# Adding an output bias to a residual held in SBUF: three VectorE additions, or two accumulating transfers that GpSimd begins

## What is computed

```python
h = concatenate([tokens(x), txt], axis=1)             # (16, 165, 256)
h = h + attn(layernorm(h))                            # y[..., None] * gelu(z) @ W_out + b_out
h = h + experts0(layernorm(h))                        # 8 experts, top 1 group, top 2
h = h + causal_attention(layernorm(h))
h = h + experts1(layernorm(h))                        # 4 experts, top 2
```

## Time and profile before

| | |
|---|---|
| Median of three runs | 919.74 us |
| The profiled execution: its time | 918.1 us |
| Its span, from the first to the last instruction | 916.1 us |
| TensorE busy | 779.2 us, 85% of the span |
| VectorE busy | 526.0 us, 57% |
| ScalarE busy | 361.0 us, 39% |
| GpSimd busy | 377.3 us, 41% |

### The profile page before, as it was taken

One profiled execution on the slowest core, in us unless ns is written; L12 is line 12 of the kernel. 1 busy time (PEld: TensorE's weight loads), 2 busy tenths in 40 slices (PEclk: granted clock), 3 DMA queues, 4 the chain that ended last, 5 costly groups with the idle time before them and its releaser, 6 DMA issues.

```text
span 916.1 us, 17558 instructions
## 1 busy us (share of the span) xinstructions
PE 779.2 (85%) x5422; PEld 612.4 (67%) x5423; DVE 526.0 (57%) x1266; ACT 361.0 (39%) x790; POOL 377.3 (41%) x322
## 2 busy tenths in 40 slices
PE   4977915999999999388999979806999999999992
PEld 3666802666666666266777758805999899899881
DVE  5996986333333333485887847693554555544550
ACT  6893761333333333233444431202444433443340
POOL 3379911232323222144555530032355555555432
PEclk9997966999999999788999987656999999999997
DMA  9930142312112121610221203031232333333325
GB/s 281 421 149 1 51 140 87 91 32 34 29 29 34 23 34 15 180 44 29 68 65 49 69 23 127 1 128 36 42 47 47 48 52 50 47 51 50 42 25 142
DMA packets 36706, 66.72 MB, mean 73 GB/s; under 512 B 3472, under 2 KB 28928, under 8 KB 34976
## 3 DMA queue, kind: packets, MB, share of 16 engines
q1 hardware_dynamic: 22656, 46.90, 15.3%
q0 software_dynamic: 13824, 19.01, 13.3%
q10 hardware_dynamic: 192, 0.38, 0.1%
HBM read 45.23 MB, written 23.74 MB: 75 GB/s over the span
## 4 chain that ended last, share of the span: by engine, by line
PE 76%; DVE 13%; POOL 4%; ACT 2%; DMA 2%; issue 1%; POOLq 0%; SPq 0%; DVEq 0%; ACTq 0%
PE PS L923 14%; PE PS L737 14%; PE PS L936 14%; PE PS L755 7%; PE PS L1230 5%; PE PS L1236 3%; PE PS L1245 2%; PE PS L745 2%; POOL X L1713 2%; PE PS L1272 2%; PE PS L2031 1%; PE PS L529 1%; PE PS L1262 1%; DVE tops L689 1%; PE PS L909 1%
## 5 line engine op out<-in xcount | busy, mean ns | idle before, releaser
L1074 POOL DMA_INDIRECT sum<-X,dest x48 | 97.1, 2023 | 108.4 <-ACT X L990 96.3
L936 PE MATMUL PS<-X 128*128 x768 | 133.5, 273 | 1.8 <-ACT X L990 1.8
L737 PE MATMUL PS<-X,Y 128*128 x576 | 134.7, 384 | 0.0
L923 PE MATMUL PS<-X 128*128 128x256 f16 x768 | 130.5, 275 | 1.6 <-DVE X L1008 1.6
L980 ACT ACTIVATE X<-PS,X 128x256 f32<-128x256 f32 x192 | 75.3, 475 | 110.3 <-PE PS L923 110.3
L923 PE MATMUL PS<-X,Y 128*128 128x256 f16 x384 | 105.7, 275 | 0.0
L936 PE MATMUL PS<-Y,X 128*128 x384 | 104.7, 273 | 0.0
L845 DVE SCALAR_TENSOR_TENSOR Y<-PS,Y 128x512 f32<-128x512 f32 x48 | 36.1, 751 | 116.0 <-PE PS L737 116.0
L895 POOL DMA_INDIRECT sum<-Y,dest x24 | 38.0, 1585 | 149.0 <-ACT Y L811 149.0
L737 PEld LDWEIGHTS PS<-X,Y 128*128 128x128 f16 x576 | 56.9, 99 | 59.3 <-issue 2.7
L923 PEld LDWEIGHTS PS<-X 128*128 x768 | 75.7, 99 | 11.5 <-issue 2.2
(11 more groups left out here) (327 smaller groups left out, 1536.0 us busy)
## 6 DMA issues: line engine op xcount, KB each, us to landing
X<-in_w_dram SPq DMA_DIRECT2D x11, 1024.0 KB, 17.2
stage<-in_w_dram SPq DMA_DIRECT2D x16, 512.0 KB, 3.6
xs<-Y SPq DMA_DIRECT2D x1, 2860.0 KB, 10.2
xs<-Y SPq DMA_DIRECT2D x2, 1419.0 KB, 6.9
sum<-h SPq DMA_DIRECT2D x1, 2816.0 KB, 9.8
h<-in_txt_dram SPq DMA_DIRECT2D x2, 1024.0 KB, 17.1
sum<-h SPq DMA_DIRECT2D x1, 2048.0 KB, 7.7
Y<-in_patches_dram SPq DMA_DIRECT2D x3, 672.0 KB, 8.1
```

The costliest lines, as they stand in the source:

```text
L737: ins = nc.tensor.matmul(PS[:, 2 * u + s, 0:F0], x_[:, slot, k, :], w_[:, at_:at_ + F0], start=(n == 0), stop=(n == 3 * KC - 1))
L923: ins = nc.tensor.matmul(PS[:, 2 * s + c // 2, (c % 2) * T1:(c % 2 + 1) * T1], part[:, off:off + P], x_[:, slot, k, :], start=(n == 0), st ...
L936: ins = nc.tensor.matmul(PS[:, 4 + a, 0:D], h_[:, s, c, a * P:(a + 1) * P], part[:, off:off + D], start=(s == 0 and c == 0 and n == 0), st ...
L1074: nc.gpsimd.indirect_dma_start(out=sum1, out_offset=bass.IndirectOffsetOnAxis(ap=dest[:, i:i + 1], axis=0), in_=y1buf[:, i // 2 % 2, i % 2 ...
```

## The change

The three additions leave VectorE's stream. GpSimd waits for `xnt_ready` (all text rows normed by ScalarE) and, as before, for `xni_ready`, and then begins two transfers from the row of `b_out` in DRAM to `h` in SBUF, one for tiles 0 to 15 and one for tiles 16 to 21, which add what they bring to what is there. The source is one row of 256 numbers (1 KB), repeated by steps of zero over 128 partitions and over the tiles. VectorE's wait ahead of L2209 is for both to have landed (32 in place of 3).

```diff
             for n in range(EARLY):
                 split(n, 4)
+            pool.wait_ge(xnt_ready, BATCH)
             pool.wait_ge(xni_ready, IT)
+            bout_row = rows_a[0:1, 5 * D:6 * D]
+            for t, n in ((0, BATCH), (BATCH, IT)):
+                nc.gpsimd.dma_start(h[:, t:t + n, :], bout_row.unsqueeze(1).broadcast_to([P, n, D]), accum_op=ALU.add)\
+                    .then_inc(bout_added, 16)
             for n in range(EARLY, XW // CW):
                 split(n, 4 if n < SCANNED else 1)
             pool_rest(pool)
...
-            def add_bout(t, n):
-
-                rows_ = h[:, t:t + n, :]
-                nc.vector.tensor_tensor(rows_, rows_, r_bout.unsqueeze(1).broadcast_to([P, n, D]), ALU.add)\
-                    .then_inc(bout_added, 1)
-            dve.wait_ge(xnt_ready, BATCH)
-            add_bout(0, 8)
-            add_bout(8, 8)
             dve.wait_ge(sp_ready, 1)
...
-            add_bout(BATCH, IT)
             dve.wait_ge(decay_ready, 1)
...
-            dve.wait_ge(bout_added, 3)
+            dve.wait_ge(bout_added, 32)
```

## The result

The kernel after takes 930.85 us (median of four runs, 929.62 to 931.04) against 919.70 us before (four runs as well): slower by a ratio of 1.0121, 95% interval 1.0098 to 1.0144, 11.1 us. The profiled execution took 929.62 us with a span of 927.5 us, against 918.1 and 916.1. So the sign and nearly the size of the forecast (934.7) came true. The cause is not the forecast's.

The account below looks back on a forecast made before the run. GpSimd's five weight chunks were taken to bound the kernel. Holding GpSimd 24.6 us for the transfers, less 9.6 us of contention, gave +15.0 us on the median 919.74: 934.7 us, range 914.5 to 949, likeliest case 928 to 940.

Parts of the forecast that it names:

- five chunks: GpSimd's weight chunks, each a rounding and a four-piece subtraction, from 52.3 to 80.1 us: 27.8 us, 18.2 in quiet.
- contention: GpSimd slowed by VectorE operations reading two SBUF operands: 9.6 us, up to 5.9 from the additions, about 3.7 the scan's.
- chunk 6: Last of GpSimd's five weight chunks, on which ScalarE, then TensorE wait: done at 80.1 us before, forecast 95.1.
- One for one: Any delay of GpSimd's last weight chunk was counted in full on round 1 and everything later: +15.0 us.
- VectorE gains almost nothing of its own: Removing VectorE's three additions (7.2 us) lets its scan start only 1.0 us earlier, off the chain of waits.
- T: Time the two transfers hold GpSimd ahead of chunk 2, from 52.3 us: taken as 24.6 us.
- lower end: Lowest transfer hold of GpSimd, without price for adding or index: 14.1 us; as rival 3, +6.5 us, 926, chance 0.20.
- the cheapest: Lowest price per 1 KB piece for GpSimd to begin transfers, from indexed rows: 0.61 us / 128 = 4.8 ns.
- The landing: Transfers' arrival in `h`, which VectorE awaits at L2209: by 80 us, covered, since TensorE needs its first pair about 101.
- rival 5: Late landing past 100 us from 2816 reads of one DRAM row; VectorE's wait replaces GpSimd's; 940 us, chance 0.05.
- Rival 1: Faster: transfers begin cheaply on GpSimd and the additions' blocking goes; at T = 2, -3.9 us, 915.8 us; chance 0.17.
- The clock: TensorE's restart at the lower 1.2 GHz level after a longer gap: at most a microsecond different, counted 0.

Follow-up runs that it names:

- e4: Kernel after, with the bias added nowhere and no transfers begun, so the bias is left out of the computation: 912.40 us, ratio 0.9923 to before.
- e1: Kernel after, with the source of both adding transfers the bias row already in SBUF on every partition: 918.51 us, ratio 0.9988 to before.
- e5: Kernel after, with SBUF source and the text tiles' transfer begun before the wait for the image rows: 915.05 us, ratio 0.9938 to before.
- e6: Kernel after, with SBUF source and one transfer of all 22 tiles in place of two: 916.44 us, ratio 0.9964 to before.
- e8: Against e5, the image tiles are added by VectorE at its old place, not by a transfer: 916.33 us, ratio 0.9958 to before.
- e9: Against e8, VectorE's addition of the image tiles is moved behind its first pair of output tiles: 915.30 us, ratio 0.9951 to before.
- e2: Kernel after, with 128 copies of the bias row in DRAM as the source, one per partition: 918.15 us, ratio 0.9984 to before.
- e10: Kernel before, with only VectorE's third addition (image tiles) moved behind its first pair of output tiles: 920.41 us, ratio 1.0000 to before.
- e3: Kernel after, same one DRAM row, but transfers overwrite `h` instead of adding, so the residual is missing: 926.27 us (one run).
- e7: Against e5, the source of both transfers is the one DRAM row, as in the kernel after: 928.93 us, ratio 1.0102 to before.

## Why the prediction was right in its number, and where it was wrong

- **What bounds the kernel: right.** GpSimd's five chunks, 9.6 us of them contention with VectorE's two-operand work, 5.9 of it by the additions: e4 measured 6.1 in chunk 6.
- **One for one with the end of chunk 6: right as a first estimate, not the whole.** To the experts' begin it held within 0.3 us for e1 (1.5 us gained in chunk 6, 1.4 there), e5 (4.0 and 3.9), e6 (2.5 and 2.4) and e8 (4.5 and 4.2). It failed for e4 (6.1 and 4.1), for e9 (6.1 and 4.2), for e2 (1.5 gained, 0.2 lost) and for e10 (1.8 gained, 1.3 lost). Two things were left out: GpSimd's later pieces can be blocked instead, and TensorE restarts at the lower clock or works on at it.
- **VectorE gains almost nothing of its own: right.** Its scan started at 67.87 against 67.94 before. With xni 0.4 us later in this execution, that is 0.5 us earlier, less than the 1.0 forecast.
- **T, the hold of GpSimd: wrong, and it carried the sum.** The step was "I take T = 24.6 us", from the indexed transfers' 1 to 2 us for every 128 pieces. It measured 4.6 us, under even the lower end of 14.1. The indexed rows' price did not carry over, for a reason that no run shows: a regular pattern cost 1.0 to 1.5 us for the instruction and 0.7 to 0.9 ns for a piece, less than a fifth of the 4.8 ns that the prediction called the cheapest. The rule of the Trainium skill that stood against it (DMA: Bandwidth & Descriptors, "Anatomy of one DMA", many descriptors before their generation shows) was the better guide here; e5 and e6 agree with it as far as the pieces go, though the begin as a whole still cost 2.1 to 4.6 us.
- **The landing: wrong.** The step was "24.6 us of the engines' time plus some 3", and therefore covered. It took 40.8 us, because the pace was set by the source row and not by the engines' work per piece, which with a good source (e1, e2) landed all in under 20 us. The same section's 2.0 us plus bytes / 436e3 would give, as an estimate, 8.6 us for the 2.9 MB; no run here comes near it, neither with the row (40.8) nor without it (18.4 at best).
- **The rivals.** The loss is rival 5 in its mechanism (2816 reads of one row; VectorE's wait at the copy of `yv` in place of GpSimd's), which had 0.05. Its landing was put past 100 us, it came at 95.5; its price was 940, since it stood on the wrong T. Rival 1's sum, -5.9 + T, gives -1.3 us with the measured T, and that is e1: 918.51, -1.2. So without the slow row the change is within 0.3% of no change.
- **The clock: under-priced.** The prediction had one gap of TensorE, longer than before, and counted 0. There were two: `o_matmul(1)` restarted at 80.97 us almost as before (3.76 us against 3.94), and the wait for the landing made a second gap of 10.7 us. The restart behind it, at the lower level, cost 2.3 us.
- **The number.** +15.0 was forecast as T - 9.6. It is -1.5 (GpSimd), overtaken by a landing that started `o_matmul(2)` 8.9 us late, plus 2.3 of clock: 11.2. That the two are close is chance.

## What to carry to other kernels

A broadcast from one short row of DRAM is not the same transfer as one from many rows: when the busy share of the DMA engines changes and the GB/s don't, ask what all the reads have in common, and take the source from SBUF or from copies. Price a transfer's begin and its landing apart, each with its own cover, and do not take the begin of a regular pattern from indexed ones. Idle time on VectorE is not free time while GpSimd works beside it: an addition moved there took 1.4 us back of the 1.8 it had given. And before a gain on one engine is passed on to the end, look whether the next engine's gap, and with it its granted clock, changes.

## What the runs showed of the hardware that was not expected

- Reading one 1 KB row of DRAM 2816 times ran at 58 to 87 GB/s, with the engines' busy share anywhere from 0.41 to 1.11. From SBUF the same pieces moved at 168 to 173 GB/s (e1, 60 to 72 us), from 128 rows of DRAM at 179 to 197 (e2).
- Adding in the transfer is no slower to land than overwriting: 40.8 and 39.6 us from the one row.
- Beginning an adding transfer of 2048 pieces and right behind it one of 768 took 2.36 and 2.44 us in GpSimd's records, which overlap; one of 768 alone took 1.46 (e5), one of 2816 alone 2.75 (e6). Without the adding (e3) the two took 0.89 and 1.41 us, and the rounding that follows 1.07 us and not 2.62.
- Adding transfers begun among the weights' loads seem to take from them: 332 GB/s were moved in all from 52 to 56 us with the one row as the source (e7) and 355 from SBUF (e5), against 426 in e1 with none of them under way until 55.6 us.
- The granted clock decides what a few us gained are worth: `o_matmul(2)` and the gate behind it took 4.0 us before, at a granted clock of 1.00, and 5.7 in e4 and e10, at 0.50 for the most part, behind a gap of 2.3 and 3.0 us.
